# Six PSUM banks and a lag of five for the expert loops, and a plain fp32 first layer for half tiles that now run ahead of the full ones

## The reference

```
h = layernorm(x) * (1 + cb) + sb                 # 4096 tokens x 256, fp32
scores = softmax(h @ Wg + bg); top 2 of 8 experts, their weights normalised
for e in range(8):
    hid = gelu(h @ W1[e] + b1[e])                # 256 -> 1024
    y   = hid @ W2[e] + b2[e]                    # 1024 -> 256
    out += y * combine_w[..., e]
x = x + gb * out
```

## Time and profile before

| | |
|---|---|
| median of 3 runs | 744.88 us (744.78 to 745.93) |
| the profiled execution's own time | 743.19 us |
| its span in the profile | 741.2 us |
| PE busy | 696.4 us, 94% of the span |
| the eight written-out tiles | to 399.39 us |
| the loops' tiles | 399.39 us to about 727.5 us |
| mean granted clock of PE | 0.979 of full speed |

### The profile page before, as it was taken

How to read it: one execution, slowest core, us unless ns; L and a number is a source line. 1 busy time by engine, 2 the same in 40 slices (tenths; PEclk the granted TensorE clock), 3 DMA queues, 4 the chain that set the end, 5 groups by cost and what they waited for, 6 DMA issues and landing times.

```text
span 741.2 us, 16152 instructions
## 1 busy us (share of the span) xinstructions
PE 696.4 (94%) x4862; PEld 637.3 (86%) x4862; DVE 507.5 (68%) x1751; ACT 421.2 (57%) x1064; POOL 401.1 (54%) x318
## 2 busy tenths in 40 slices
PE   5799999999999999998999999999999999999992
PEld 2578888788888888898899999999899999999992
DVE  5879889998888794766645565466775565566451
ACT  4556564656555555656445575565666566575560
POOL 1165537786765765556735255454655364464443
PEclk9899999999999998999999999999999999999997
DMA  8361011202204124365534353675643555433333
GB/s 297 121 226 53 6 57 66 94 32 85 88 15 152 65 74 117 89 147 135 106 74 72 62 126 59 128 178 134 168 71 71 134 112 126 77 61 68 67 72 44
DMA packets 50604, 72.79 MB, mean 98 GB/s; under 512 B 5968, under 2 KB 42396, under 8 KB 50528
## 3 DMA queue, kind: packets, MB, share of 16 engines
q0 software_dynamic: 16480, 27.28, 20.5%
q1 hardware_dynamic: 34048, 44.60, 19.2%
HBM read 48.85 MB, written 23.01 MB: 97 GB/s over the span
## 4 chain that ended last, share of the span: by engine, by line
PE 77%; DVE 9%; issue 5%; DMA 4%; ACT 2%; POOL 2%; DVEq 0%; SPq 0%; another core or an unknown queue 0%; POOLq 0%; ACTq 0%
PE mm L1097 23%; PE yb L1107 23%; PE mm L988 19%; PE yb L1013 6%; PE tp L1088 3%; DMA out_x<-ysb,tokb 1%; DMA gbr<-mod_rows,xm 1%; DVE ytmp L1554 1%; DMA h2all<-in_L_wmod 1%; PE tp L1003 1%; DVE ysb L1562 1%; PE tp L1024 1%; DMA mb<-mod_rows 1%; DVE hl L1533 1%; DVE ob L1311 1%
## 5 line engine op out<-in xcount | busy, mean ns | idle before, releaser
L917 ACT ACTIVATE hh<-mm,vT 128x256 fp32r<-128x256 f32 (+1 forms) x288 | 135.6, 471 | 155.2 <-PE mm L1097 123.6
L663 POOL DMA_INDIRECT out_x<-ysb,tokb x68 | 110.6, 1627 | 183.8 <-DVE ysb L1562 142.9
L1533 DVE TENSOR_TENSOR hl<-mm,hh 128x256 fp32r<-128x256 f32 (+1 forms) x288 | 116.5, 407 | 115.0 <-ACT mm L918 88.2
L1097 PE MATMUL mm<-fh,SH 128*128 128x256 f32 x576 | 166.6, 289 | 13.2 <-DVE hl L1533 7.4
L1097 PE MATMUL mm<-fl,SH 128*128 128x256 f32 x576 | 162.5, 282 | 0.1
L1097 PE MATMUL mm<-fh,SL 128*128 128x256 f32 x576 | 162.3, 282 | 0.0
L1107 PE MATMUL yb<-SH,hh 128*128 128x256 f32 x544 | 157.1, 289 | 0.5 <-issue 0.5
L1107 PE MATMUL yb<-SH,hl 128*128 128x256 f32 x544 | 154.0, 283 | 0.8 <-issue 0.8
L1107 PE MATMUL yb<-SL,hh 128*128 128x256 f32 x544 | 153.8, 283 | 0.3 <-issue 0.3
L918 ACT ACTIVATE mm<-mm,vT 128x256 f32<-128x256 f32 (+1 forms) x288 | 126.9, 441 | 0.0
L1097 PEld LDWEIGHTS mm<-fh,SH 128*128 128x128 f32 x576 | 110.5, 192 | 17.8 <-DVE hl L1533 9.8
(11 more groups left out here) (232 smaller groups left out, 1163.4 us busy)
## 6 DMA issues: line engine op xcount, KB each, us to landing
xin<-disp_x SPq DMA_DIRECT2D x74, 132.0 KB
wraw<-in_L_ffn_W SPq DMA_DIRECT2D x8, 1024.0 KB
h2all<-in_L_ffn_W SPq DMA_DIRECT2D x8, 1024.0 KB
xb<-in_L_attn_x SPq DMA_DIRECT2D x8, 512.0 KB, 7.1
out_x<-x2b SPq DMA_DIRECT2D x8, 512.0 KB
mb<-mod_rows SPq DMA_DIRECT2D x3, 768.0 KB, 6.1
wraw<-in_L_attn_W_ugg SPq DMA_DIRECT2D x1, 1536.0 KB, 11.8
gbr<-mod_rows,xm POOLq DMA_INDIRECT x74
```

Source lines behind the costliest of these rows:

```text
L663: e.indirect_dma_start(out=out_rows, out_offset=bass.IndirectOffsetOnAxis(ap=tokb[:, j:j + 1], axis=0), in_=ysb[:, j, :], in_offset=None, ...
L917: e.activation(hh[:, f, c_], mm[f % 4][:, c_], ACT.Gelu_apprx_tanh, bias=bias)
L1097: i = e.matmul(mm[f % 4][:, 0:TE], a[:, k, f * 128:(f + 1) * 128], b[:, k, :], start=(k == 0 and t == 0), stop=(k == 1 and t == 2))
L1533: e.tensor_tensor(hl[:, f, w_], mm[f % 4][:, w_], hh[:, f, w_].bitcast(F32), ALU.subtract)\
```

## The change

- `more_tiles` runs the half tile ahead of the loop of full tiles. So it follows the expert's first tile (for expert 0 the last written-out tile). SP takes 128 off its position after a half tile, and DVE moves its window of places by 128 instead of 256.
- A half tile's first layer is `layer1_half`: two plain fp32 matmuls a chunk, of 128 columns, from the raw W1 in `wraw` and a new buffer `fr`, which ACT copies from `rowsT` at the tile's start, after `fl` is made. PE waits for that copy (`rows_raw`).
- In the loops the first layer uses six banks (`mm[0..3]`, `yb[1]`, `tp[1]`), and layer2 runs 5 chunks behind in full and half tiles alike. The wait for `hidden` moves from layer1 to layer2.
- Since W1's raw form is read until the half tile is over, SP loads it one expert later: W1 of n + 1 in expert n's first tile. W1 of expert 2 moves from the written-out tiles into the loops.

```
         def more_tiles(e, rs, n, tile):
             k, half = count_of(e, rs, n)
+            with e.If_ne(half, 0):
+                tile(False, 1)
             with e.Fori(0, k):
                 tile(False, 2)
-            with e.If_ne(half, 0):
-                tile(False, 1)
...
+        def bank(f, late):
+            return (mm + [yb[1], tp[1]])[f % 6] if late else mm[f % 4]
...
 (SP, written-out tiles)
-                if i == 2:
+                if i == 3:
                     split_done(e, 0)
-                    load_w1(2)
-                if i == 3:
                     load_w2(2)
 (SP, loops)
                     load(n)
-                    if first and n + 2 < E:
-                        split_done(e, n)
-                        load_w1(n + 2)
+                    if parts == 1:
+                        e.reg_add(r_pos, r_pos, -128)
+                    if first and n + 1 < E:
+                        split_done(e, n - 1)
+                        load_w1(n + 1)
...
                 if n and n + 2 < E:
+                    split_done(e, n)
                     load_w2(n + 2)
 (ACT, loops)
                 def tile(first, parts):
+                    if parts == 1:
+                        due("rows_low")
+                        e.activation(fr[:, :, :], rowsT[:, :, 0:128], ACT.Copy).then_inc(S["rows_raw"], 1)
                     for f in range(NF):
-                        gelu(n, f, parts)
+                        gelu(n, f, parts, True)
 (PE)
-            def layer1(n, f):
+            def layer1(n, f, late=False):
...
-                if f >= 4:
+                if f >= 4 and not late:
                     due("hidden_low", 1)
...
+            def layer1_half(n, f):
+                w1 = wraw[n % 2][:, 0:2048].rearrange("p (c n) -> p c n", c=2)
+                for k in range(2):
+                    i = e.matmul(bank(f, True)[:, 0:128], w1[:, k, f * 128:(f + 1) * 128], fr[:, k, :], start=(k == 0), stop=(k == 1))
+                i.then_inc(S["layer1_done"], 1)
...
-            def layer2(n, f, parts):
+            def layer2(n, f, parts, late=False):
-                if f >= 4:
+                if f >= 4 or late:
                     due("hidden_low", 1)
 (PE, a loop's tile)
-                    lag = 4 if parts == 2 else 6
+                    if parts == 1:
+                        due("rows_raw", 1)
+                    lag = 5
                     for f in range(NF):
-                        layer1(n, f)
+                        if parts == 2:
+                            layer1(n, f, True)
+                        else:
+                            layer1_half(n, f)
                         if f == lag:
                             due("y_taken", 1)
                         if f >= lag:
-                            layer2(n, f - lag, parts)
-                    layer2(n, NF - lag, parts)
+                            layer2(n, f - lag, parts, True)
+                    layer2(n, NF - lag, parts, True)
                     turn()
                     for f in range(NF - lag + 1, NF):
-                        layer2(n, f, parts)
+                        layer2(n, f, parts, True)
 (DVE, loops)
-                        hidden(f, parts)
+                        hidden(f, parts, True)
```

More of the change, by code:

```diff
@@ L180, in build @@
         ytmp = sb(ctx, "ytmp", [128, 2, D])
+        fr = sb(ctx, "fr", [128, 2, 128])
         x2f = x2b[:, :, :, :].rearrange("p a j d -> p (a j d)")
@@ L731, in act_program @@
         def act_program(e):
-            due, grow, to_registers = counter(e, "act", ("layer1_done", "layer2_done", "rows_turned"))
+            due, grow, to_registers = counter(e, "act", ("layer1_done", "layer2_done", "rows_turned", "rows_low"))
             def weights_high(part, k):
@@ L843, in high_rows @@
                 e.activation(fh[:, :, :], rowsT, ACT.Copy).then_inc(S["rows_high"], 1)
+                grow("rows_low", 1)
             e.wait_ge(S["const_made"], 4)
@@ L910, in act_program, with gelu @@
                         split_high(e, 0, q)
-            def gelu(n, f, parts):
+            def gelu(n, f, parts, late=False):
                 c_ = slice(0, 128 * parts)
+                u = bank(f, late)[:, c_]
                 due("layer1_done", 1)
@@ L916, in gelu @@
                 bias = vT[:, n * NF + f:n * NF + f + 1]
-                e.activation(hh[:, f, c_], mm[f % 4][:, c_], ACT.Gelu_apprx_tanh, bias=bias)
-                e.activation(mm[f % 4][:, c_], mm[f % 4][:, c_], ACT.Gelu_apprx_tanh, bias=bias)\
+                e.activation(hh[:, f, c_], u, ACT.Gelu_apprx_tanh, bias=bias)
+                e.activation(u, u, ACT.Gelu_apprx_tanh, bias=bias)\
                     .then_inc(S["gelu_done"], 1)
@@ L970, in pe_program @@
         def pe_program(e):
-            due, grow, to_registers = counter(e, "pe", ("hidden_low", "y_taken", "rows_loaded", "rows_low"))
+            due, grow, to_registers = counter(e, "pe", ("hidden_low", "y_taken", "rows_loaded", "rows_low", "rows_raw"))
             def main_part(g, hc, part):
@@ L1096, in layer1 @@
                     for t, (a, b) in enumerate(((w1h, fh), (w1h, fl), (w1l, fh))):
-                        i = e.matmul(mm[f % 4][:, 0:TE], a[:, k, f * 128:(f + 1) * 128], b[:, k, :],
+                        i = e.matmul(bank(f, late)[:, 0:TE], a[:, k, f * 128:(f + 1) * 128], b[:, k, :],
                                      start=(k == 0 and t == 0), stop=(k == 1 and t == 2))
                 i.then_inc(S["layer1_done"], 1)
-            def layer2(n, f, parts):
+            def layer1_half(n, f):
[4 more added lines that the diff above has]
+            def layer2(n, f, parts, late=False):
                 w2h, w2l = (t[n % 2][:, 2048:4096].rearrange("p (c n) -> p c n", c=NF) for t in (SH, SL))
-                if f >= 4:
+                if f >= 4 or late:
                     due("hidden_low", 1)
@@ L1528, in mark, with hidden @@
                 ins.then_inc(S["dve_d"], 1)
-            def hidden(f, parts):
+            def hidden(f, parts, late=False):
                 w_ = slice(0, 128 * parts)
                 due("gelu_done", 1)
-                e.tensor_tensor(hl[:, f, w_], mm[f % 4][:, w_], hh[:, f, w_].bitcast(F32), ALU.subtract)\
+                e.tensor_tensor(hl[:, f, w_], bank(f, late)[:, w_], hh[:, f, w_].bitcast(F32), ALU.subtract)\
                     .then_inc(S["hidden_low"], 1)
@@ L1635, in tile @@
                     for f in range(NF):
-                        hidden(f, parts)
-                        row_weights(f, float((n + 1) * CAP), lambda: e.tensor_scalar(nom[:, :], nom[:, :], float(TE), None, ALU.add))
+                        hidden(f, parts, True)
+                        row_weights(f, float((n + 1) * CAP), lambda: e.tensor_scalar(nom[:, :], nom[:, :], float(128 * parts), None, ALU.add))
                         if first and n + 1 < E:
```

2 lines of the change are left out of this document (1 added, 1 removed).

## The result

The changed kernel takes 732.51 us (median of 4 runs, 730.45 to 733.90) against 744.83 us for the kernel before (4 runs, 744.18 to 745.93): ratio 0.9839, 95% interval 0.9814 to 0.9864. The profiled execution took 730.45 us with a span of 728.5 us, where the one before had 743.19 and 741.2.

What follows compares the result with a forecast made beforehand. PE, busy 94% of the span, was taken to bound the kernel. Gains of 7.5 us (half tiles) and 3.5 us (banks, lag) made 11.0 off 743.19, 732.2; plus 1.7 to the median gave 733.9 us, range 728 to 740.

Steps and rivals of the forecast that it cites:

- likeliest case: The forecast's own case for the whole kernel: 733.9 us, spanning 731 to 737 us; chance 0.52.
- stalls in full tiles (banks, lag): In full tiles, 1.44 us more patience for `hidden` cuts stalls of 3.74 us to 0.22: 3.5 us gained.
- written-out tiles: Tiles ahead of the loops: the load taken out of them was counted as nothing.
- my list of seven places: Idle places of PE in the loops before: two wait for `fl`, five for `hidden`; each costs its idle plus 0.16 us.
- The half tile by itself: Half tile's PE work: 32 fp32 matmuls at 0.108 us replace 48 at 0.12; 6.8 us with second layer and transposes.
- the rival of the full 0.216 us: Half tile's first layer: fp32 gets no cheaper with fewer columns, half tile 10.2 us, kernel 742.2 us; chance 0.07.
- What a half tile is worth: Gate rows landing late set each half tile's charge, 8.13 us; four make 32.5 against 40.0 before: 7.5 us gained.
- T + 12.45: PE's earliest restart in the tile behind a half one, in us; T is the end of the tile before the half tile.
- the rival in which nothing holds the half tile: Gathers land earlier, so a half tile costs its 6.8 us: 5.3 us more gain, 728.6 us; chance 0.10.
- my sign of being wrong: In the profile after, half tiles taking over 8 us on PE would show the prediction wrong.
- The clock: Rival: PE's clock falls to 1.2 GHz behind each half tile's stall, giving back 4.8 us: 738.7 us; chance 0.12.
- POOL and W1: Rivals: late gathers stall a second tile behind half tiles, 737.9 us, chance 0.11; late W1 holds DVE, 746.5 us, chance 0.08.

Runs made afterwards that it cites:

- experiment 5: The changed kernel again, unaltered, against the kernel before on another chip: 714.74 us, ratio 0.9815.
- experiment 8: The changed kernel with a lag of four chunks instead of five, six banks kept: 721.12 us, ratio 0.9906 to the kernel before, 6.4 us behind the changed kernel.
- experiments 2: The kernel before with only the order changed (half tile ahead of the loop; four banks, lags 4 and 6, three products): 724.52 us, ratio 0.9976.
- 3: The changed kernel with four banks and the old lags 4 and 6, keeping order and fp32 form: 725.36 us, ratio 0.9989 to the kernel before.
- 11: The changed kernel with two spare buffer fills on POOL ahead of the gathers in each expert's first tile: 745.60 us, ratio 1.0037 to the kernel before.
- experiment 9: The changed kernel a third time, unaltered, against the kernel before on a third comparison's chip: 729.89 us, ratio 0.9841.
- experiment 6: The changed kernel with both gathers issued ahead of the first add on POOL in the loops: 763.85 us, ratio 1.0498 to the kernel before.
- experiment 10: The changed kernel with a 1 MB memory copy queued ahead of W1's load in the loops' first tiles: 745.62 us, ratio 1.0054 to the kernel before.
- experiment 12: The changed kernel with a half tile waiting only for its own gather, its result made ahead of the next metadata: 730.20 us, ratio 0.9834 to the kernel before.

## Why the prediction was right

The forecast (733.9 us, sum 11.0 us) and its likeliest case held. Taken apart by the profile's own stretches, the loops' tiles take 328.0 us instead of 341.8 (from 400.48 instead of 399.39 to the end of the spans), 13.8 us less:

| term | forecast | measured |
|---|---|---|
| stalls in full tiles (banks, lag) | 3.5 | 3.7 |
| four half tiles with the stalls behind them | 7.5 | 6.6 |
| full tiles without their stalls | 0 | 3.5 |
| written-out tiles | 0 | -1.1 |
| sum | 11.0 | 12.7 |

That the sum came so close is in part luck: the 3.5 us that I had at nothing is set against 0.9 us less from the half tiles and 1.1 us lost ahead of the loops.

**Six banks, lag five.** The stalls of 1.58, 0.50 and 1.66 us are gone: all 3.7 us, where I left 0.2 of the last. In the second profile of the same kernel (experiment 5) one is back, 0.56 us idle in a full tile of expert 2. What the lag saves beyond the three places shows only when it is taken away (experiment 8: 6.4 us).

**Full tiles without their stalls.** This was no term of my sum. By the row below of the kernel before, three full tiles of even experts took 34.93 us; after, three such take 34.40.

```profile
668.26:703.19 34.93, 34.93 (x302) 34.82 (x301) 19.06 (x63) 20.31 (x51) 15.54 (x12) 1.00 0.40 69
```

Over the 13 full tiles of even experts it is 2.6 us, and the other full tiles give 0.9. The start times in the kernel before place most of it. Here PE waits for `hidden` ahead of the fifth chunk:

```profile
544.70 0.28 PE L1097 MATMUL mm<-fh,SL 128*128 128x256 f32 x1
545.12 0.39 PE L1097 MATMUL mm<-fh,SH 128*128 128x256 f32 x1
545.35 0.28 PE L1097 MATMUL mm<-fl,SH 128*128 128x256 f32 x1
```

The starts are 0.42 and 0.23 us apart where 0.12 is the rule, and no idle time stands in brackets, since a row of 0.28 us hides it. Twelve full tiles have such a short wait at this place, 1.9 us in all, which my list of seven places left out. The five listed waits cost 0.1 us each more than I priced, as the interval behind the waiting matmul is 0.22 us too. In the full tiles after, only two short waits are left, 0.2 us of them not charged to a half tile. So about 2.2 of the 3.5 us are the same patience at `hidden`, a term that I had too small by that. In the rest, the matmuls of even experts simply stand closer: their intervals are 0.113 to 0.114 us in some stretches of a tile and 0.117 to 0.119 in others, and fewer are of the second kind after. This isn't tied to the six banks alone: with four banks (experiments 2 and 3) expert 0's first full tile takes 11.49 us, the others 11.57 or more, and with six banks four of the 13 still take 11.62 us or more. Why is open.

**The half tile by itself.** Right. The fp32 matmuls in PE's timeline after:

```profile
402.37 0.61 PE L1114 MATMUL yb<-fr,wraw 128*128 128x128 f32 x4
402.81 0.61 PE L1114 MATMUL tp<-fr,wraw 128*128 128x128 f32 x4
```

Four in 0.44 us are 0.11 us each (0.112 by the start times over a tile) where I took 0.108, and half tiles are 7.12 us of PE where I had 6.8. Of the 0.3 us between them 32 x 0.0035 = 0.11 is fp32's. The start times around the tile from 445.32 place the rest: its second matmul comes 0.21 us behind the first, and the next tile's first 0.26 us behind its last, since `fl` is made at 452.38 only. That ends the rival of the full 0.216 us. ACT's new copy took 0.39 us, ahead of the tile, as expected; it ended 0.05 to 0.6 us ahead of the tile, so its cover is thin.

**What a half tile is worth.** Right in kind: PE restarts at T + 12.52 us behind one half tile, where the sum went by T + 12.45. That close a match is luck: the landing came at T + 10.69, 0.34 us later than I took, and from there to PE's restart it was 1.83 us instead of 2.1. Of the stalls of 1 to 1.5 us that I expected behind each half tile, one came (1.17 us, the others 0.56, 0.27 and 0.10). DVE's timeline shows the landings it waited for:

```profile
456.12 0.17 DVE L1320 TENSOR_REDUCE xm<-xin 128x16 f32<-128x16 f32 x1 [3.74 <-DMA gbr<-mod_rows,xm]
...
558.42 0.17 DVE L1320 TENSOR_REDUCE xm<-xin 128x16 f32<-128x16 f32 x1 [2.90 <-DMA gbr<-mod_rows,xm]
...
612.02 0.17 DVE L1320 TENSOR_REDUCE xm<-xin 128x16 f32<-128x16 f32 x1 [2.48 <-DMA gbr<-mod_rows,xm]
```

They are T + 10.80, T + 10.34 and T + 9.56, each 0.1 us behind its landing: I took 10.35 for the landing from two, and the spread is larger than I gave it. Charges of 8.29, 8.06 and 7.23 us against 8.13 follow. The third is nearly the rival in which nothing holds the half tile. Experiments 3 and 11 show the mechanism from both sides: shorten PE's work without giving patience, and nothing comes; bring the gathers 2.6 us later and PE's restart is 2.3 us later (T + 14.37 after T + 12.04 in experiment 9). The mis-sized part is expert 0's half tile, 9.86 us where I charged 8.13. It follows the last written-out tile, at the place where the kernel before has 1.42 us of stall, and I wrote that what is left of that stall lies in this half tile, but gave it no price. It was 1.17 us shown, and `fl` was late by 0.58 at its end. This half tile is also 9.59 us long; of that PE is busy for 7.61, so my sign of being wrong (over 8 us on PE) is met by its length and not by its work.

**The clock.** It stayed at 1.00 behind the loops' stalls, of up to 1.17 us; in no experiment did an idle time of 1.0 to 1.66 us in the loops have a fall behind it either. The rival was a real mechanism, met only behind longer stalls: in experiments 3, 6, 10 and 11 the granted clock fell behind eleven of the twelve idle times above 2 us (2.08 to 5.30 us; the twelfth was 2.46 us), as in this stretch of 3 us behind the longest, in experiment 6:

```profile
488.43:491.43 3.00, 3.00 (x14) 3.00 (x15) 3.00 (x11) 0.00 (x0) 2.07 (x3) 0.50 0.12 26
```

14 matmuls in it are 0.21 us apart. The rule of the Trainium skill (TensorE: Matmul & The Clock Gate, "A second HAM failure mode: psum-queue depth-cycling"), by which small gaps between groups of matmuls can make the clock swing, would have given 738.7 us; this kernel's gaps of up to 1.17 us didn't.

**POOL and W1.** No second stall follows a half tile. In none of the twelve profiles does DVE wait for a weight load in the loops, at 15.0 us between issue and use neither. Both had real prices near them, but on other ways: experiment 6 shows what a POOL that is behind costs (49 us), and experiment 10 what late adds cost.

**Written-out tiles.** They ended 1.1 us later, in one profile each; in experiments 9, 10 and 12 the changed loops begin at 400.38, 400.32 and 399.88. As the change leaves out a load there, I take it for spread, which isn't shown. Against it, in the other two comparisons too the kernels with the later W1 begin their loops no earlier than those without (385.08 us against 384.68 to 385.05, and 385.16 to 385.65 against 383.84), so a small cost of the change there isn't ruled out.

## What to carry to other kernels

Price a saving on the bound engine against the chain of the others before counting it: here the whole worth of the fp32 layer hung on 1.44 us more patience at one wait, and without it the same edit gave nothing that could be measured (21.13 us for the pair of tiles in both kernels). Find when that chain ends, relative to a fixed point (T + 12.45 us), and subtract what PE has to do until then. The idle time that a profile shows is not the whole of PE's waits: read the start times too, for those that a row's length hides. And where indirect adds follow one another, what goes ahead of them on their queue can cost far more than what goes behind (49 us in experiment 6).

## What the runs showed of the hardware that I had not expected

- An undisturbed full tile of an odd expert takes 11.95 us in every kernel, one of an even expert 11.46 or 11.47 us (nine of 13 in the changed kernel). Less 0.45 of transposes and over 96 matmuls that is 0.120 us apart for the experts of one set of weight buffers and 0.115 for those of the other, and the second is a mean: 0.113 to 0.114 in some stretches, 0.117 to 0.119 in others. Why is not shown.
- A wait of PE costs 0.1 us beyond itself: the interval behind the waiting matmul is 0.22 us instead of 0.12 (544.70 to 545.35 in the kernel before).
- Halving the columns of an fp32r matmul from 256 to 128 took it from 0.120 to 0.112 us with an odd expert's weights and from 0.114 to 0.112 with an even one's; for a plain fp32 one, which shows as two instructions, from 0.216 to 0.112 us each.
- After a stall of 2.8 us the lower clock held for 3.5 us: the stall cost half as much again as it showed.
- In the chains of waits the indirect adds took 3.9 to 5.4 us in experiment 12, and up to 8.09 us in experiment 10, with another megabyte queued; experiment 6 has one of 7.95 us without it.
- The written-out tiles ended at about 385 us in the runs of the first two comparisons and at 400 in the third, for kernels that don't differ there but ran on different chips; the time of the kernel before moved with it (726 and 728 against 742 us). Up to the first of these tiles (280 us) the profiles agree within 2 us. In the eight tiles the mean granted clock was 1.00 in the first two and 0.96 in the third. Whether that is cause or consequence of the stalls there is not shown.
